# Turning the second eight heads of eleven items on VectorE, and moving two small jobs to GpSimd, in a two-layer cross-attention kernel

## The reference, cut to what matters

```
x: (16, 128, 512)   ctx: (16, 128, 512)   H = 512, 16 heads of 32
layer 0:  x += attention(layernorm(x) -> q, k, v; mask 128x128) @ w_ao      stage A
          x += attention(q from layernorm(x); k, v from ctx; mask) @ w_co   stage B
          x += gelu(layernorm(x) @ w1) @ w2                                 MLP
layer 1:  a = layernorm(ctx);  Q = x @ Wq.T;  K = a @ Wk.T;  V = a @ Wv.T   stage D
          P = softmax(Q K.T / sqrt(32), masked keys at -inf)
          x + tanh(gate) * (P V) @ Wo.T                                     (gated attention)
```

## Time and profile before

| | |
|---|---|
| median of 3 runs | 1100.44 us (1100.13 to 1104.86) |
| span of the profiled execution | 1100.7 us |
| TensorE busy | 1074.7 us, 98% of the span |
| VectorE, ScalarE, GpSimd busy | 815.4, 712.7, 462.0 us |
| moved by DMA, mean over the span | 152 GB/s |

### The profile page before, as it was taken

The page is one execution under the profiler, slowest core; times in us unless marked ns, Lnnn a source line. Parts: engine busy times, 40 slices in busy tenths (PEclk is TensorE's granted clock), DMA queues, the critical chain, the costliest instruction groups (busy, mean ns, idle before and its releaser), DMA issues.

```text
span 1100.7 us, 24328 instructions
## 1 busy us (share of the span) xinstructions
PE 1074.7 (98%) x8829; PEld 934.2 (85%) x8829; DVE 815.4 (74%) x1314; ACT 712.7 (65%) x2365; POOL 462.0 (42%) x337
## 2 busy tenths in 40 slices
PE   7989999999999999998999999999999999999998
PEld 6888888888888888886898888888888988888886
DVE  6678787778888778888877557656677478778777
ACT  4678777777788778786444434434444387777776
POOL 3665666557767776767512121103012331122100
PEclk9999999999999999999999999999999999999999
DMA  6366565576776777553241130220622146666633
GB/s 216 98 201 198 191 195 188 174 227 216 221 227 215 223 211 229 180 191 128 85 134 40 38 96 12 85 96 1 181 101 83 59 146 205 203 198 210 177 97 97
DMA packets 136135, 167.04 MB, mean 152 GB/s; under 512 B 16992, under 2 KB 82256, under 8 KB 136016
## 3 DMA queue, kind: packets, MB, share of 16 engines
q1 hardware_dynamic: 136016, 165.50, 47.9%
HBM read 113.15 MB, written 52.29 MB: 150 GB/s over the span
## 4 chain that ended last, share of the span: by engine, by line
PE 59%; DVE 12%; ACT 9%; POOL 7%; issue 4%; DMA 3%; SPq 1%; DVEq 0%; ACTq 0%; POOLq 0%
PE psum L938 15%; PE psum L919 14%; PE psum L758 13%; POOL prob L2023 6%; PE psum L858 5%; PE psum L750 5%; ACT prob L1217 4%; ACT prob_blocks L1217 2%; PE psum L794 2%; PE psum L776 2%; DVE prob L1590 2%; DVE ln_tile L1528 2%; PE psum L835 2%; DVE negmax L1603 2%; ACT inputs_transposed L1255 2%
## 5 line engine op out<-in xcount | busy, mean ns | idle before, releaser
L758 PE MATMUL psum<-inputs_hi,weights_hi 128*128 128x256 f32 x768 | 223.7, 291 | 5.4 <-POOL inputs_lo L2014 2.5
L758 PE MATMUL psum<-inputs_lo,weights_hi 128*128 128x256 f32 x768 | 217.1, 283 | 0.0
L758 PE MATMUL psum<-inputs_hi,weights_lo 128*128 128x256 f32 x768 | 217.0, 283 | 0.0
L2014 POOL TENSOR_TENSOR inputs_lo<-inputs_transposed,inputs_hi 128x512 fp32r<-128x512 f32 x84 | 113.0, 1367 | 228.9 <-DVE inputs_hi L1563 168.4
L2023 POOL TENSOR_TENSOR prob<-prob,mask_bias 128x1024 f32<-128x1024 f32 x64 | 152.7, 2408 | 98.3 <-DVE prob L1590 96.3
L1217 ACT ACTIVATE prob<-prob,negmax 128x128 f32<-128x128 f32 x472 | 182.2, 391 | 0.5 <-DVE negmax L1603 0.5
L758 PEld LDWEIGHTS psum<-inputs_hi,weights_hi 128*128 128x128 f32 x768 | 146.7, 191 | 10.3 <-issue 2.8
L1603 DVE TENSOR_REDUCE negmax<-prob 128x8 f32<-128x1024 f32 x96 | 115.9, 1210 | 50.0 <-POOL prob L2023 50.0
L758 PEld LDWEIGHTS psum<-inputs_lo,weights_hi 128*128 128x128 f32 x768 | 147.0, 191 | 0.2
L758 PEld LDWEIGHTS psum<-inputs_hi,weights_lo 128*128 128x128 f32 x768 | 146.9, 191 | 0.0
L858 PE MATMUL psum<-weights_hi,context_parts 128*128 128x512 f32 x376 | 125.8, 393 | 0.4 <-ACT kT L1168 0.3
(11 more groups left out here) (124 smaller groups left out, 2600.3 us busy)
## 6 DMA issues: line engine op xcount, KB each, us to landing
prob_turned<-prob_blocks SPq DMA_DIRECT2D x37, 512.0 KB, 3.0
prob<-prob_turned SPq DMA_DIRECT2D x148, 128.0 KB, 3.3
weights_whole<-weights_in SPq DMA_DIRECT2D x72, 256.0 KB, 3.4
normalised<-ln_tile SPq DMA_DIRECT2D x30, 512.0 KB, 2.8
inputs_transposed<-normalised SPq DMA_DIRECT2D x120, 128.0 KB, 2.9
context<-row_sums_spread SPq DMA_DIRECT2D x188, 64.0 KB, 2.1
stream<-residual SPq DMA_DIRECT2D x42, 256.0 KB, 2.7
residual<-stream SPq DMA_DIRECT2D x42, 256.0 KB, 3.7
```

The lines of the kernel that those rows point to most:

```text
L758: mm = pe.matmul(ps[:, bank, GT * part:GT * part + GT], w[:, slot, c, o], a[:, buf, c, :], start=c == 0 and i == 0, stop=c == KC - 1 and i ...
L2014: pool.tensor_tensor(lo, y, hi.bitcast(f32), ALU.subtract).then_inc(s_rlo if fill.ln is None else s_flo, 1)
```

## The change

Items 33 to 43 (`WHOLE`) now take the block route for all sixteen heads. The exps of heads 8 to 15 go to a second tile, VectorE turns it in the next step, SP stores it and brings it back. TensorE no longer transposes anything for these items and ScalarE no longer copies them. `row_sums` uses another PSUM bank for them. For items 32 to 43 GpSimd makes the low parts of the context, and in all of stage D it makes the layer norm's normalisation. Semaphores, tiles and a few bank waits follow from that. The core of the diff:

```diff
+WHOLE = tuple(range(33, 44))
+LO_BY_POOL = tuple(range(32, 44))
         def row_sum_bank(g):
-            return U_BANK if sums_late(g) else U_BANK + 1
+            return T_BANK + 1 if g in WHOLE else U_BANK if sums_late(g) else U_BANK + 1
 # SP
+            def store_second_blocks(g):
+                n = second_number(g)
+                sp.wait_ge(s_turned2, n)
+                if n > 2:
+                    sp.wait_ge(s_moved2, 64 * (n - 2))
+                sp.dma_start(turned_second[n % 2], second_blocks[:, :]).then_inc(s_pst2, 16)
+            def bring_second_blocks(g):
+                n = second_number(g)
+                sp.wait_ge(s_pst2, 16 * n)
+                blocks = turned_second[n % 2].rearrange("(i k) (j n) -> j k i n", i=4, j=4)
+                for j in range(4):
+                    dst = prob[32 * j:32 * j + 32, g % 2, NH // 2 * T:].rearrange("p (i n) -> p i n", i=4)
+                    sp.dma_start(dst, blocks[j]).then_inc(s_moved2, 16)
                 if st.prev and g - 1 not in BY_PE:
                     bring_blocks(g - 1)
+                if g - 1 in WHOLE:
+                    store_second_blocks(g - 1)
                 if st.prev:
                     store_row_sums(g - 1)
                 if st.ends:
                     load_stream(g - 2)
                 if st.later and st.later.ln is not None and not ahead_ln and g:
                     load_tiles(st.later)
+                if g - 1 in WHOLE:
+                    bring_second_blocks(g - 1)
                 if st.prev:
                     spread_row_sums(g - 1)
 # TensorE: row_sums, times_v, step
-                if sums_late(g):
+                if g in WHOLE:
+                    pe.wait_ge(s_cx, 2 * g)
+                elif sums_late(g):
-                pe.wait_ge(s_pta, copied_by_act(g, 1))
+                if g in WHOLE:
+                    pe.wait_ge(s_rc, g + 1)
+                    pe.wait_ge(s_moved2, 64 * second_number(g))
+                else:
+                    pe.wait_ge(s_pta, copied_by_act(g, 1))
-                    else:
+                    elif g - 1 not in WHOLE:
                         transpose_prob(g - 1, 2)
                         if g != 44:
                             transpose_prob(g - 1, 3)
                 if not late:
-                    if st.prev:
+                    if g - 1 in WHOLE:
+                        u_bank_free(g)
+                    elif st.prev:
                         row_sums_out(g - 1)
-                if g == 44:
+                if g == 44 and g - 1 not in WHOLE:
                     transpose_prob(g - 1, 3)
 # ScalarE: exps, step
+                second = g in WHOLE and quarter >= 2
+                if second and quarter == 2 and second_number(g) > 1:
+                    act.wait_ge(s_pst2, 16 * (second_number(g) - 1))
-                elif st.prev and g != 44:
+                elif st.prev and g != 44 and g - 1 not in WHOLE:
                     probs_out(g - 1)
 # VectorE
+            def turn_second_blocks(g):
+                dve.wait_ge(s_exp, 4 * g + 4)
+                dve.transpose(second_blocks[:, :], second_blocks[:, :]).then_inc(s_turned2, 1)
                 if st.ends and not late:
                     inverse_sums(g - 1)
+                if g - 1 in WHOLE:
+                    turn_second_blocks(g - 1)
+                if st.ends and not late and g - 2 not in LO_BY_POOL:
                     context_lo(g - 2, 0)
                     context_lo(g - 2, 1)
-                if ahead_ln and later_ln:
+                if ahead_ln and later_ln and phase != D:
                     normalise(st.ahead)
 # GpSimd
+            def normalise(fill):
+                pool.wait_ge(s_rstd, 2 * fill.n + 2)
+                for t in range(GB):
+                    pool.tensor_scalar(lnx[:, t, :], lnx[:, t, :], mv[:, t, 0:1], rstd[:, t:t + 1],
+                                       ALU.subtract, ALU.mult).then_inc(s_xhat, 1)
+            def context_lo(g, h):
+                half = slice(256 * h, 256 * h + 256)
+                pool.wait_ge(s_chi, 2 * g + h + 1)
+                pool.tensor_tensor(clo[0][:, half], ctxn[:, half], chi[0][:, half].bitcast(f32), ALU.subtract).then_inc(s_clo, 1)
             def step(st):
                 phase, b, g = st.phase, st.b, item(st)
+                if g - 2 in LO_BY_POOL:
+                    context_lo(g - 2, 0)
+                    context_lo(g - 2, 1)
+                if phase == D and st.ahead and st.ahead.ln is not None:
+                    normalise(st.ahead)
```

More of the change, by code:

```diff
@@ L151, with second_number, turned_by_pe @@
 BY_PE = (0, 27, 28, 29, 30, 31, 32, 44, 45, 46, 47)
+WHOLE = tuple(range(33, 44))
+LO_BY_POOL = tuple(range(32, 44))
 def moved_number(g):
     return g + 1 - sum(k <= g for k in BY_PE)
+def second_number(g):
+    return sum(k <= g for k in WHOLE)
+def turned_by_pe(k):
+    return 4 if k in BY_PE else 0 if k in WHOLE else 2
 def transposed_count(g, c):
-    return sum(4 if k in BY_PE else 2 for k in range(g)) + (c + 1 if g in BY_PE else c - 1)
+    return sum(turned_by_pe(k) for k in range(g)) + (c + 1 if g in BY_PE else c - 1)
 def copied_by_act(g, half):
-    return sum(2 if k in BY_PE else 1 for k in range(g)) + (half + 1 if g in BY_PE else 1)
+    return sum(turned_by_pe(k) // 2 for k in range(g)) + (half + 1 if g in BY_PE else 1)
 def copied_by_dve(g, half):
@@ L297, in build @@
         turned = nc.dram_tensor("prob_turned", (2, 128, NH // 2 * T), f32, kind="Internal").ap()
+        turned_second = nc.dram_tensor("second_prob_turned", (2, 128, NH // 2 * T), f32, kind="Internal").ap()
         spread = nc.dram_tensor("row_sums_spread", (4, KC * T), f32, kind="Internal").ap()
@@ L319, in build @@
         s_moved = sem("prob_blocks_moved")
+        s_pst2 = sem("second_prob_blocks_stored")
+        s_moved2 = sem("second_prob_blocks_moved")
         s_scores = sem("scores")
@@ L362, in build @@
         s_turned = sem("prob_blocks_turned")
+        s_turned2 = sem("second_prob_blocks_turned")
         s_clo = sem("ctx_lo")
@@ L813, in row_sums_out, with u_bank_free @@
                 pe.wait_ge(s_rc, g + 1)
+            def u_bank_free(g):
+                if g - 1 in (1, 33):
+                    half_out(g // 16, 1, 4)
+                else:
+                    stream_out(g - 3)
             def times_v(g):
                 phase, q, gp, half = g // 16, (g % 16) // 2, (g // 2) % 2, g % 2
-                pe.wait_ge(s_pta, copied_by_act(g, 1))
+                if g in WHOLE:
+                    pe.wait_ge(s_rc, g + 1)
+                    pe.wait_ge(s_moved2, 64 * second_number(g))
+                else:
+                    pe.wait_ge(s_pta, copied_by_act(g, 1))
                 if g in BY_PE:
@@ L831, in times_v @@
                         P = prob[:, g % 2, T * h:T * h + T]
-                        if h < NH // 2 and g not in BY_PE:
-                            P = by_head(prob[:, g % 2, 0:NH // 2 * T])[:, h]
+                        if (h < NH // 2 and g not in BY_PE) or g in WHOLE:
+                            eight = h // 8 * NH // 2 * T
+                            P = by_head(prob[:, g % 2, eight:eight + NH // 2 * T])[:, h % 8]
                             out = out.rearrange("p (i q) -> p i q", q=32)
@@ L1214, in exps @@
                     dst = src
-                    if moved:
-                        dst, src = by_head(pblocks[:, :])[:, s], src.rearrange("p (j k) -> p j k", k=32)
+                    if moved or second:
+                        blocks = second_blocks if second else pblocks
+                        dst, src = by_head(blocks[:, :])[:, s % 8], src.rearrange("p (j k) -> p j k", k=32)
                     ins = act.activation(dst, src, ACT.Exp,
@@ L1728, in step @@
                 mask_scores(g, 1)
-                if late:
+                if late and g - 2 not in LO_BY_POOL:
                     context_lo(g - 2, 0)
@@ L1765, in step @@
                     prob_out(g - 1, 3)
-                if ahead_ln and not later_ln and st.ahead != mlp_fill(0):
+                if ahead_ln and not later_ln and st.ahead != mlp_fill(0) and phase != D:
                     normalise(st.ahead)
```

1 line of the change is left out of this document (added).

## The result

The changed kernel takes 1127.28 us (median of 4 runs, 1126.23 to 1133.44) against 1100.33 us: ratio 1.0244, 95% interval 1.021 to 1.0278. It is slower, as forecast, but by 27 us where 10 were forecast, and outside the range that was given. The profiled execution has a span of 1124.8 us, 24.1 more than before; the other 2.9 of the 27 us lie between the profiled executions and the medians of the runs, and no row speaks of them.

The account below looks back on a forecast made before the run. TensorE's matmuls were taken as the bound, with SP's DMA chain adding waits after the change. The terms sum to +10.0 us, the 8.7 us saved already included, giving 1110.5 us, range 1093 to 1119.

Parts of the forecast that it names:

- The saving: TensorE in steps 34 to 44: eight transposes dropped per step, 0.79 us each of eleven times, 8.7 us in all.
- Where the new wait stands: times_v waits for the fetched second blocks, some 3 us at the starts of steps 36, 38, 40, 42, 44, and at 45.
- Step 34: VectorE's second turn delays the reciprocal by 1.25 us; with the saved transposes and no wait after, together +0.5 us.
- the even step's chain: Turn, store and fetch through SP's queue: store at 5.6, last block landing at 13.7 us, just when TensorE wants it; no wait.
- the odd step: SP's store at 7.6 lands at 12.0, last block at 16.8 us against 13.8 wanted: TensorE waits 3.0 us.
- The sum: Steps 34 to 44: four pairs +5.6, step 43 +2.2, step 44 +1.7, step 34 +0.5, total +10.0 us.
- The DMA engines become the bound: Rival: 1.05 MB more a step raises the odd step's DMA share to 0.94 and stretches landings; 1120 us, chance 0.12.
- Its own signs: Waits of some 3 us at odd steps' ends, odd steps 16 to 17 us, even near 13.7, odd DMA share above 0.85.
- Cost nothing: GpSimd's added low parts and normalisation, 4.2 us in an even step, hidden in the 9.13 us it waits there.
- I had taken 1.4: GpSimd's layer-norm normalisation in even steps: 1.4 us for each tile, with a range of 0.5 to 2.8.
- 4 us for two dependent DMAs: Side rule from the skill's about 2.0 us fixed per DMA: two dependent ones never below 4 us; not used in the sum.

Follow-up runs that it names:

- e4: The changed kernel with 36 identity transposes ahead of times_v in steps 36, 38, 40, 42 and 44, keeping TensorE busy while it waits: 1.0249 of the kernel before.
- e9: As e5, but every second store and fetch moves an eighth of the bytes, with the same issues, waits and turn: 1.0141 of the kernel before.
- e10: As e5 with all bytes, but each fetch takes what the step before stored, so SP does not stand still: 1.0159 of the kernel before.
- e12: The changed kernel with only items 35, 39 and 43 turned whole and GpSimd's small jobs back on VectorE: 1.0109 of the kernel before.
- e1: The changed kernel without any item turned whole, only GpSimd's small jobs kept: 1.0022 of the kernel before.
- e5: The kernel before with VectorE's second turn and the new DMA traffic added, TensorE and ScalarE unchanged and not waiting for it: 1.0228 of the kernel before.

## Why the prediction was right in its mechanism and wrong in its size

- *The saving.* 0.79 us for each of eleven steps, TensorE's work 13.7 and 13.8 us: right (13.70 in e4, 13.78 after).
- *Where the new wait stands.* The starts of steps 36, 38, 40, 42, 44, at a step's end that SP reaches through two landings: right (3.98, 3.68, 5.24, 4.16, 3.61 us). At step 45, where 2.5 us were forecast, it is 0.45: the time is in step 44 itself, 14.97 us, at a clock of 0.81.
- *Step 34.* Forecast +0.5; 16.64 against 16.07 us. Its wait for the row sums grew from 1.39 to 2.74 us, as said.
- *The step that failed* is the even step's chain: "I take 5.6", and then "The store lands 3.3 later (median) at 8.9; four issues end at 10.8; the last, issued at 10.3, lands 3.4 later at 13.7. TensorE wants it at 13.7: no wait." The last block of steps 36, 38, 40 and 42 landed at 14.8 to 15.4, not 13.7. Two terms were too small. The first is the place of the store, 6.0 to 6.7 in these steps (mean 6.5). 5.6 was the end of the turn alone, but the store also stands behind `bring_blocks`, and in the even step of the kernel before SP leaves that at 6.7, as its row in step 36 (start 924.12) shows. Afterwards SP left it at 5.7 to 6.6, and the turn itself ended at 6.0 to 6.6:

```profile
928.83 1.96 SPq L525 DMA_DIRECT2D prob<-prob_turned  x4
```

- The second term is the landing of that store, 3.8 to 4.3 us (mean 4.1), not 3.3. The 3.3 was of a stage that moved 1.05 MB a step less: the DMA share rose from 0.60 and 0.72 to 0.70 to 0.82. These two, 0.9 and 0.8 us, and 0.3 us of issues make `store_normalised` go out at 15.0 on the mean, not 13.0. In the odd step the two landings were sized right (4.1 for the normalised rows, 4.2 for the store where 4.4 was taken); `bring_blocks` came 0.8 us later than its sum and the fetched blocks 0.5. The odd step's last block landed 17.3 to 18.9 us into it, not 16.8. Together a pair is 33.6 us (steps 36 to 43), not 30.5.
- *The sum.* Four pairs gave 134.6 - 4 x 29.09 = +18.2 (forecast 5.6), step 43 +2.8 (2.2), step 44 +2.5 (1.7), step 34 +0.6 (0.5), together 24.1 us, the whole difference of the two spans.
- *The rivals.* "The DMA engines become the bound" (1120, chance 0.12) came nearer in time than the forecast did, but not by its condition: it was to decide from a share near 0.9, and no step went above 0.82. e9 shows bytes at 0.9% of time in the traffic test; e10 shows that standing still is nearly as much. It was a mistake to set the two as alternatives, with chances of their own: a stage whose bytes grow by over a third and whose queue grows by a serial landing has both.
- *Its own signs.* The waits stood where it said. Even steps "near 13.7" and odd ones of "16 to 17 us" did not come (15.1 to 15.8 and 17.4 to 19.0), nor did a DMA share above 0.85 in the odd steps (0.70 to 0.82).
- *The clock* was not in the prediction. After each wait TensorE ran at the lower level for some microseconds. e4 shows that this costs 2 us at most here, e12 that it costs 1.5 to 2.7 us where the next step isn't bound by the same chain.
- *GpSimd.* "Cost nothing": 1.0022 (e1), within what was called no change. Its own time was mis-sized, though: see below.

## What to carry to other kernels

A row's latency holds for the traffic of its own stage, and a place in a queue for its own step: take each from the step in which the new issue will stand. When a change adds bytes and a dependent pair of transfers to a queue that already fills the step, price the landings at the upper end of their rows, multiply by the number of them in the loop, and ask what is behind each wait. When the step of the loop is set by such a chain, work removed from the busiest engine returns as idle time, and keeping its clock up gains little. Before calling a wait the cause, run the new traffic without the wait: here the kernel took the same time. And before calling a queue the cause, look at the landings in the queue that replaces it.

## What the runs showed of the hardware that was not expected

- GpSimd's normalisation, a tensor-scalar form of 128x512, takes 2.1 us, where VectorE takes 0.5 and I had taken 1.4. Timeline of GpSimd after:

```profile
930.30 1.45 POOL L2091 TENSOR_TENSOR context_parts<-context,context_parts 128x256 fp32r<-128x256 f32 x2 [1.51 <-ACT context_parts L1299]
931.73 4.16 POOL L2070 TENSOR_SCALAR ln_tile<-ln_tile,ln_mean_var,ln_rstd 128x512 f32<-128x512 f32 x2
```

- Beside GpSimd's two-input work, VectorE's small scalar form stretches threefold, to about the time of one of GpSimd's own instructions (0.69 against 1.45 for two). The same line of VectorE after, with GpSimd busy from 930.30 to 931.75, and in the next step, where GpSimd began at 946.61:

```profile
930.41 0.69 DVE L1634 TENSOR_SCALAR mask_bias<-mask_rows 128x128 f32<-128x128 uint8 x1
...
946.48 0.23 DVE L1634 TENSOR_SCALAR mask_bias<-mask_rows 128x128 f32<-128x128 uint8 x1 [1.12 <-DMA mask_rows<-mask_d_in]
```

- A store of 64 KB in place of 512 KB (e9, in smaller pieces) landed after 3.5 us on the median, against 4.4 in e5: an eighth of the bytes takes off a fifth of the latency. The 16 KB fetches of e9 landed after 1.8 us on the median, so a landing can take less than the 2.0 us on which the prediction's 4 us for two dependent DMAs was built.
- The same dependent store and fetch land later when GpSimd or ScalarE issues them (4.9 and 3.7 us) than when SP does (4.4 and 2.9), rows above. No run shows why.
